# Attention stage of a graph network: visits in pairs of one node block, new orders on four engines, scatters without a bound

## The reference

```python
feat = jnp.concatenate([x[src], edge_weights, x[dst]], axis=1)      # 144 columns
h = jax.nn.relu(feat @ W_att1.T + b_att1)
scores = (h @ W_att2.T + b_att2)[:, 0]
m = jax.ops.segment_max(scores, src, num_segments=num_nodes)
e = jnp.exp(scores - m[src])
denom = jax.ops.segment_sum(e, src, num_segments=num_nodes)
msg = jax.ops.segment_sum((e / denom[src])[:, None] * lin_x[dst], src, num_segments=num_nodes)
```

## Time and profile before

| | us |
|---|---|
| median of 3 runs | 6971.01 |
| runs, lowest to highest | 6955.53 to 6972.53 |
| the profiled execution | 6953.3 |
| its span, first to last instruction | 6951.5 |

### The profile page before, as it was taken

How to read it: one execution, slowest core, us unless ns; L and a number is a source line. 1 busy time by engine, 2 the same in 40 slices (tenths; PEclk the granted TensorE clock), 3 DMA queues, 4 the chain that set the end, 5 groups by cost and what they waited for, 6 DMA issues and landing times.

```text
span 6951.5 us, 172751 instructions
## 1 busy us (share of the span) xinstructions
PE 4916.4 (71%) x30025; PEld 3702.1 (53%) x30026; DVE 4522.2 (65%) x20036; ACT 2115.2 (30%) x5541; POOL 4929.4 (71%) x10449
## 2 busy tenths in 40 slices
PE   6444777777545766676666666666888888888887
PEld 2334444444434544455445444444777777777775
DVE  5777888888434743333333333335999999999997
ACT  4000000000000432222222222223555555555555
POOL 1677777777777367777777777776777777777775
PEclk9555555555555777767877787776888888888888
DMA  8333333333333143333333333334333333333333
GB/s 270 67 60 60 57 60 60 57 60 60 64 60 61 62 133 111 111 110 109 105 106 105 106 106 105 106 105 128 95 94 94 95 95 95 94 94 95 95 95 93
DMA packets 1146496, 649.15 MB, mean 93 GB/s; under 512 B 798450, under 2 KB 1050340, under 8 KB 1145573
## 3 DMA queue, kind: packets, MB, share of 16 engines
q1 hardware_dynamic: 1006804, 412.21, 24.3%
q0 software_dynamic: 137728, 233.30, 11.8%
q10 hardware_dynamic: 1888, 2.83, 0.2%
HBM read 360.75 MB, written 311.42 MB: 97 GB/s over the span
## 4 chain that ended last, share of the span: by engine, by line
issue 19%; PE 15%; POOL 14%; DVE 8%; DMA 4%; ACT 3%; POOLq 1%; DVEq 1%; ACTq 0%; SPq 0%
PE banks L1397 7%; POOL rows_by_src L832 6%; DMA rows_by_src<-ring 3%; PE banks L1443 3%; DVE wide L1991 2%; DVE wide L1996 1%; DVE ring L2002 1%; ACT ring L1085 1%; ACT ring L1092 1%; POOL ring L893 1%; PE banks L1398 1%; PE banks L1385 1%; PE banks L1434 1%; DVE ring L1947 1%; PE banks L1458 1%
## 5 line engine op out<-in xcount | busy, mean ns | idle before, releaser
L832 POOL DMA_INDIRECT rows_by_src<-ring x1760 | 1711.7, 973 | 553.1 <-issue 488.5
L804 POOL DMA_INDIRECT wide<-msg_table,ring x1664 | 1578.8, 949 | 632.1 <-issue 419.4
L1397 PE MATMUL banks<-wide,ring 128*128 x3520 | 1281.9, 492 | 473.6 <-ACT ring L1085 403.4
L1311 PE MATMUL banks<-wide,ring 128*128 x3520 | 859.5, 426 | 505.7 <-DVE acc L1764 190.9
L1397 PEld LDWEIGHTS banks<-wide,ring 128*128 128x128 f32 x3520 | 742.5, 261 | 746.6 <-issue 696.2
L1311 PEld LDWEIGHTS banks<-wide,ring 128*128 128x128 f32 x3520 | 784.7, 328 | 584.0 <-issue 583.5
L1092 ACT COPY ring<-banks 128x416 f32<-128x416 f32 x880 | 402.2, 510 | 1448.8 <-PE banks L1398 1448.8
L1958 DVE COPY ring<-ring 128x4 f32<-128x4 f32 x440 | 80.1, 182 | 1145.5 <-DMA rows_by_src<-ring 1145.4
L1443 PE MATMUL banks<-wide,ring 128*128 x5328 | 708.6, 262 | 0.0
L1764 DVE TENSOR_TENSOR acc<-acc,banks 128x64 f32 x1760 | 388.8, 221 | 366.0 <-DVE acc L1764 201.8
L1443 PEld LDWEIGHTS banks<-wide,ring 128*128 128x128 bf16 x5328 | 544.1, 108 | 114.2 <-issue 0.2
(11 more groups left out here) (326 smaller groups left out, 9426.3 us busy)
## 6 DMA issues: line engine op xcount, KB each, us to landing
wide<-rows_by_src SPq DMA_DIRECT2D x1776, 105.0 KB, 2.0
ring<-attr_turned SPq DMA_DIRECT2D x440, 128.0 KB
attr_turned<-ring SPq DMA_DIRECT2D x416, 96.0 KB
rows_by_src<-ring POOLq DMA_INDIRECT x1760
wide<-msg_table,ring POOLq DMA_INDIRECT x1664
ring<-attr_by_dst SPq DMA_DIRECT2D x208, 64.0 KB
attr_turned<-ring SPq DMA_DIRECT2D x208, 64.0 KB
attr_by_dst<-in_edge_attr_dram SPq DMA_DIRECT2D x1, 13281.2 KB
```

The lines of the kernel that those rows point to most:

```text
L804: g.indirect_dma_start(out=A_g[:, b * GV + u, :], out_offset=None, in_=table[:, :], in_offset=bass.IndirectOffsetOnAxis(ap=A_idx[:, b * GV ...
L832: g.indirect_dma_start(out=rows_d[:, :], out_offset=bass.IndirectOffsetOnAxis(ap=B_pos[:, s, u:u + 1], axis=0), in_=B_row[:, s, u, :], in_ ...
L1311: last = mm(bank[s][:, u * HID:(u + 1) * HID], A_D[:, s, u, :], A_g[:, ds(r[u], 1), :].rearrange("p a k -> p (a k)"), start=True, stop=True)
L1397: mm(b, B_DT[:, t, u, :], qh[:, w, :].rearrange("p a k -> p (a k)"), start=True, stop=False)
```

## The change

The visits of the attention stage come in pairs of one block. A block with an odd number of visits gets one more, whose lanes all lie outside. The stage's table is made for 98 more visits (1872 instead of 1776), so the pipeline has 78 turns of six steps, 468 steps, instead of 74 and 444. The maximum, its correction and the sums are then kept by pair: two columns instead of four, two additions to `acc` instead of four, and TensorE accumulates the two sums of a pair in PSUM. The penalties are worked out once, ahead of the stage (`pens`), and GpSimd copies twelve columns of them once in six steps.

In each engine's `tick` the order is new. On VectorE the comparison moves from the head of the turn behind the scan; on TensorE the transposes of the one-hot matrix move behind the turn of the scores; the product of rows and `C_p` goes from GpSimd (one operation of 128x260) to ScalarE (four of 128x65), and ScalarE's two large copies move to the end of its turn.

For the scatters, the bound goes away. `rows_by_src` gets 16 x 128 spare rows, and a lane outside the block writes the spare row that `aside` names.

The diff, cut to its core:

```diff
-C_VISITS = C_BODY * -(-VISITS // C_BODY)
+C_VISITS = C_BODY * -(-(-(-N_EDGES // P) + N_WIN - 1 + N_WIN) // C_BODY)
+PV = GV // 2
-        rows_d = dram("rows_by_src", [SLOTS, ROW])
+        rows_d = dram("rows_by_src", [SLOTS + BODY * P, ROW])
...
# GpSimd, send
-                            in_=B_row[:, s, u, :], in_offset=None, bounds_check=SLOTS - 1, oob_is_err=False).then_inc(b_sc[s], 16)
+                            in_=B_row[:, s, u, :], in_offset=None).then_inc(b_sc[s], 16)
...
# GpSimd, tick
-                    m_pen = ch.do(g.tensor_tensor(C_pen[:, s, :], wbase_all[:, ds(n, GV)], wbase[:, ds(n, GV)], ALU.subtract))
+                    if s == 3:
+                        after_c(pool, c_new, CS - 1, i, CS)
+                        g.tensor_copy(C_pen, pens[:, ds(i * (CS * PV), CS * PV)]).then_inc(c_pen, 1)
...
-                    m_r = ch.do(g.tensor_tensor(C_r[:, t, :], C_s[:, t, :], sp_[0], ALU.subtract))
-                if 0 in stages:
-                    ch.need(m_pen)
-                    g.tensor_tensor(C_pen[:, s, :], C_pen[:, s, :], C_step, ALU.mult).then_inc(c_pen, 1)
-                if 2 in stages:
-                    ch.need(m_r)
+                    ch.link(g.tensor_tensor(C_r[:, t, :], C_s[:, t, :], sp_[0], ALU.subtract))
...
-                    after_c(pool, c_p, t, j)
-                    after_c(pool, c_ag, t, j, 2)
-                    g.tensor_tensor(C_W[:, t % 2, :, :], C_V[:, t, :, H1:ROW_SRC],
-                                    per_group(C_p[:, t, :], HID + 1), ALU.mult).then_inc(c_W, 1)
...
# ScalarE, tick
+                    after_c(act, c_p, t, j)
+                    after_c(act, c_ag, t, j, 2)
+                    for u in range(GV):
+                        last = a.activation(C_W[:, t % 2, u, :], C_V[:, t, u, H1:ROW_SRC], ACT.Identity, scale=C_p[:, t, u:u + 1])
+                    last.then_inc(c_W, 1)
...
# TensorE, tick: the sums of a pair
-                        last = mm(bank[6 + t % 2][:, u * (HID + 1):(u + 1) * (HID + 1)], C_S[:, t, u, :], C_W[:, t % 2, u, :],
-                                  start=True, stop=True)
+                        last = mm(bank[6 + t % 2][:, (u // 2) * (HID + 1):(u // 2 + 1) * (HID + 1)], C_S[:, t, u, :], C_W[:, t % 2, u, :],
+                                  start=u % 2 == 0, stop=u % 2 == 1)
...
# VectorE, visit_table and rows
+                    ch.link(v.tensor_scalar(ei, t1, 1.0, None, ALU.add))
+                    ch.link(v.tensor_scalar(ei, ei, 1, None, ALU.arith_shift_right))
+                    ch.link(v.tensor_copy(t1, ei))
+                    v.scalar_tensor_tensor(nt[0:K, :], t1, 2.0, hs, ALU.mult, ALU.mult).then_inc(s_vcols, 1)
...
-                    ch.link(v.scalar_tensor_tensor(B_sh[:, s, :], B_rec[:, s, :, 1], -BIG, B_in[:, s, :], ALU.add, ALU.mult))
+                    ch.link(v.tensor_tensor(B_sh[:, s, :], B_rec[:, s, :, 1], aside[:, s, :], ALU.subtract))
+                    ch.link(v.tensor_tensor(B_sh[:, s, :], B_sh[:, s, :], B_in[:, s, :], ALU.mult))
...
+            ch.link(v.tensor_tensor(pens, of_pairs(wbase_all[:, 0:C_VISITS]), of_pairs(wbase), ALU.subtract))
+            v.tensor_scalar(pens, pens, MASKED / P, None, ALU.mult).then_inc(c_init, 1)
```

More of the change, by code:

```diff
@@ L337, in build @@
         C_kl = part(ring, CS * GV // 2, RING).bitcast(bf16).rearrange("p (s u) -> p s u", s=CS)
-        C_mp = part(ring, CS * GV * PARTS // 2, RING).bitcast(bf16).rearrange("p (s u k) -> p s u k", s=CS, u=GV)
-        C_raw, C_s, C_r, C_pen, C_mo, C_mr, C_df, C_cr, C_mg, C_z, C_d, C_p = (marks(CS) for _ in range(12))
-        C_zero, C_step = part(ring, GV, RING), part(ring, GV, RING)
-        C_mn = part(ring, 1 + CS * GV, RING)
+        C_mp = part(ring, CS * PV * PARTS // 2, RING).bitcast(bf16).rearrange("p (s u k) -> p s u k", s=CS, u=PV)
+        C_raw, C_s, C_r, C_mg, C_z, C_d, C_p = (marks(CS) for _ in range(7))
+        C_mo, C_mr, C_df, C_cr = (part(ring, CS * PV, RING).rearrange("p (s u) -> p s u", s=CS) for _ in range(4))
+        C_pen = part(ring, CS * PV, RING)
+        pens = part(ring, C_VISITS // 2, RING)
+        C_zero = part(ring, GV, RING)
+        C_mn = part(ring, 1 + CS * PV, RING)
         at[0] = 0
@@ L1417, in tick @@
                     for u in range(GV):
[L1418 removed]
+                        last = mm(bank[5][:, u * PARTS:(u + 1) * PARTS], C_STb[:, t, u, :], C_mp[:, t, u // 2, :], start=True, stop=True)
                     last.then_inc(c_mm, 1)
@@ L1429, in tick @@
                     last.then_inc(c_MKt, 1)
-                if 0 in stages:
-                    after_c(pe, c_N, s, i)
-                    after_c(pe, c_STc, s, i, 1)
-                    for u in range(GV):
-                        last = tr(bank_b[0][:, u * P:(u + 1) * P], C_N[:, s, u, :], ident_b[:, :])
-                    last.then_inc(c_St, 1)
                 if 1 in stages:
@@ L1451, in tick @@
                     tr(bank_b[1][0:PARTS * GV, 0:P], C_parts[:, t, :], ident_b[:, :]).then_inc(c_pt, 1)
+                if 0 in stages:
+                    after_c(pe, c_N, s, i)
+                    after_c(pe, c_STc, s, i, 1)
+                    for u in range(GV):
+                        last = tr(bank_b[0][:, u * P:(u + 1) * P], C_N[:, s, u, :], ident_b[:, :])
+                    last.then_inc(c_St, 1)
                 if 5 in stages:
```

131 lines of the change are left out of this document (67 added, 64 removed).

## The result

The changed kernel takes 7233.16 us in the median (7225.5 to 7240.5), the kernel before beside it 6971.77: a ratio of 1.038 (95% interval 1.036 to 1.040), 3.8% slower.

The account below looks back on a forecast made before the run. VectorE was taken to set the attention stage's pace, GpSimd's issue rate the scatters'; a ScalarE-GpSimd ring would become the new bound. 6953.3 + 390 - 25 + 2 = 7320, with 17.7 for the median 7338 us; range 7060 to 7420.

Parts of the forecast that it names:

- More steps: Attention stage: 468 steps instead of 444, which at the old pace alone would cost 109 us.
- VectorE's own turn, 4.07: Attention stage: VectorE's work per step falls from 4.54 to 4.07 us; as the bound it would give 1921 us.
- the rival in which the multiplications vanish in ScalarE's idle time: Attention stage: the ring does not close and VectorE stays the bound, 6837 us in all; chance 0.10.
- its 0.47 for two additions: VectorE in the attention stage: dropping two additions to the sums removes spacings of 0.25 and 0.22 us per step.
- The ring of 4.59: Attention stage: ScalarE and GpSimd wait for each other in a closed path, making 4.59 us the step's lower limit.
- The meeting, 0.55: Attention stage: VectorE's comparison holds up a GpSimd operation each step, adding 0.55 us, for a step of 5.14.
- The two paths that were to end 0.01 apart: Attention stage: from the small copy's start, comparison 1.99 us behind and GpSimd's first operation 2.00, so they meet.
- its rival: Attention stage: comparison and GpSimd operation do not meet, the step stays 4.59 us, 7080 in all; chance 0.17.
- Scatters without a bound, 25 of 0 to 49: Edge-row scatters: dropping the bound saves up to 28 ns on each of 1760, 0 to 49 us; 25 taken.
- SP's refills of the rows, costed at nothing: Attention stage: refilling row slots after ScalarE's signal has over 9 us of time, so costs nothing.
- TensorE at its lower level: Attention stage: TensorE stays at 1.2 GHz, its own turn 5.0 us, 7272 in all without the meeting; chance 0.05.
- The 2 us of the tables: Ahead of the attention stage: five small operations and two over 936 columns add an estimated 2 us.

Follow-up runs that it names:

- experiment 9: Changed kernel, ScalarE still multiplying the rows, with the old orders of VectorE, ScalarE and TensorE, row 0 to 127 in SBUF: 6834.73 us, ratio 0.982.
- experiment 12: Changed kernel with old engine orders, ScalarE multiplying, row 0 to 127 in PSUM, and block-number table on partition 0 instead of 64: 6834.12 us, ratio 0.982.
- experiment 1: Changed kernel with the comparison reading the row 0 to 127 from PSUM instead of SBUF: 7041.84 us, ratio 1.011.
- experiment 2: Changed kernel with the comparison reading the row 0 to 127 as 4-byte instead of 2-byte numbers from SBUF: 7226.72 us, ratio 1.038.
- experiment 6: Changed kernel with row multiplication on GpSimd and all engine orders as before, leaving the pairs of visits and scatters without a bound: 7152.97 us, ratio 1.027.
- experiment 7: Changed kernel with GpSimd's row multiplication and all engine orders as before, plus the row 0 to 127 in PSUM: 7162.03 us, ratio 1.027.
- experiment 4: Changed kernel with the row multiplication back on GpSimd and the new orders kept: 7085.09 us, ratio 1.018.
- experiment 8: Changed kernel, ScalarE still multiplying, with the old orders of VectorE, ScalarE and TensorE and the row 0 to 127 in PSUM: 6848.14 us, ratio 0.982.
- experiment 3: Changed kernel with one 128x260 multiplication on ScalarE instead of four of 128x65, all four visits taking the first's weight: 6964.21 us, ratio 1.001.
- experiment 5: Changed kernel with the row multiplication back on GpSimd, new orders kept, and the row 0 to 127 in PSUM: 7047.98 us, ratio 1.010.
- experiment 11: Kernel before the change with the comparison reading the row 0 to 127 from PSUM: 6965.53 us, ratio 0.999.
- experiment 10: Changed kernel with ScalarE's first 128x512 copy put back ahead of the exponentials, all else as changed: 7240.55 us, ratio 1.040.

## Why the prediction was right, and where its sizes were off

The forecast was slower, by a ring through ScalarE and GpSimd with one held operation in each turn, at 7338. It came out slower by that mechanism, at 7233, 105 less. The step accounts for 108 less and the scatters, which gave nothing, for 25 more; the last 22 less are the spread of runs, since the forecast put the median 18 above the profiled execution and it lies 4 below. That the last two nearly cancel is luck. The steps of the prediction:

- **More steps:** 468, as counted.
- **VectorE's own turn, 4.07:** not the bound in the changed kernel. Where the ring is open and VectorE is the bound (experiment 9) a step takes 4.066, and the kernel 6835; the rival in which the multiplications vanish in ScalarE's idle time was priced at 6837. So the condition of that price isn't met in the changed kernel, because of its orders and not because of the multiplications as such. That the price agrees to 2 us is luck: it holds 25 us for the scatters that weren't there, and its 0.47 for two additions is two misses that partly cancel. VectorE in experiment 9:

```profile
5522.34 0.16 DVE L2034 TENSOR_REDUCE ring<-banks 128x4 f32<-128x12 f32 x1
5522.42 0.69 DVE L2038 TENSOR_REDUCE banks<-banks 128x2 f32<-128x512 f32 x1
```

Against the earlier trace rows the time from one of these to the other falls from 0.45 to 0.08 where the prediction took 0.25 away, and that from the scan to the first addition of the node's part from 0.46 to 0.14 (5523.21 to 5523.35) where it took 0.22. On average over the stage the two are worth 0.59, not 0.47, and 0.15 of it goes again into the longer load (experiment 12), which the prediction had put behind the scores.
- **The ring of 4.59:** there, and all its links are seen in the timelines. It measures 4.475 in the median and 4.50 in the mean (experiment 1). Score copies to GpSimd 0.55 (0.56 predicted), GpSimd's chain to the exponential 1.38 (1.35). The mis-sized part is from the exponential to the next score copies, medians over the stage 2.55 instead of 2.68: exponential 0.24 instead of 0.28, multiplications 0.98 instead of 0.96, then in the timeline above 0.14 from the small copy to the first large one (0.21 predicted), 0.63 and 0.57 (0.63, 0.60). The small copy had been sized by the spacing of the two score copies, and the second large copy at 0.60 where the prediction's own rows give 0.67 - 0.09 = 0.58.
- **The meeting, 0.55:** it happens in nearly every turn, as forecast, and costs 0.405. Expected was the first operation, L868; held were L869, L870 or L877, L868 hardly ever (its median stays 202 ns). The two paths that were to end 0.01 apart do not: L868 comes 1.89 behind the small copy's start (2.00 predicted), the comparison 1.96 in the shortest turns (1.99 predicted) but 2.21 in the median and up to 3.05, because VectorE waits for TensorE on the way there (L2005 and L2031 in the waits above). So L868 begins 0.07 to 1.15 ahead of the comparison and gets through, and one of the operations behind it is caught. One that begins later behind the comparison's start loses less: L869, begun 0.16 behind it, loses 0.40, L877, begun 0.20 behind it, 0.35. The prediction allowed for this in a sentence (0.3 to 0.5) and then summed 0.55; the meeting holds over so wide a shift because the chain is longer than the comparison, as the prediction said against its rival. The Trainium skill (GPSIMD Engine Reference, Key points) says that GpSimd contends with VectorE instructions of two SBUF inputs; experiments 1 and 2 agree, 4.50 with one such input and 4.90 with two. Together the two terms, 4.50 and 0.41, make 4.91 instead of 5.14, and 468 x 0.23 = 108 us of the sum.
- **Scatters without a bound, 25 of 0 to 49:** 0. The median is 972 ns with and without a bound, and 1760 of them take 2248.5 us from first to last start (before 2250.9). So the 28 ns against the gather aren't the bound's; whether the length of the rows makes them wasn't tried. VectorE's additional work there (838 busy instead of 783 us) comes out of its waiting, 1075.0 us for landed scatters instead of 1145.4, and costs nothing, as predicted. The Trainium skill (DMA: Bandwidth & Descriptors, Anatomy of one DMA) calls the cost of making descriptors small; the unchanged 972 agrees as far as the bound goes, and what the 972 ns themselves are spent on no run here shows.
- **SP's refills of the rows, costed at nothing:** nothing. GpSimd waits for rows 32.4 us in five cases, 27.4 of it ahead of the first step and the last case 61 us behind it.
- **TensorE at its lower level:** it ran at it more often, 0.75 of full clock in the stage instead of 0.87, and a step from comparison to comparison varies between 4.0 and 5.9 us with it. But it doesn't set the pace. Four successive turns, cut at ScalarE's score copies (the column behind POOL is the clock):

```profile
5407.15:5412.14 4.99, 3.43 (x37) 2.67 (x37) 3.78 (x17) 3.09 (x12) 2.83 (x12) 0.97 0.33 86
5412.14:5416.95 4.81, 4.47 (x34) 4.07 (x35) 3.33 (x15) 3.08 (x12) 2.72 (x12) 0.50 0.36 90
5416.95:5422.11 5.16, 4.10 (x43) 3.51 (x41) 4.33 (x19) 3.09 (x13) 2.67 (x12) 0.83 0.33 83
5422.11:5427.06 4.95, 4.62 (x35) 4.24 (x36) 3.46 (x16) 3.08 (x13) 2.90 (x12) 0.50 0.37 87
```

A turn at 1.2 GHz (0.50) isn't longer than one at 2.4: over the stage the 150 turns with at least three quarters of their time at 1.2 GHz last 4.88 on average, the 139 with as much at 2.4 GHz 4.94. Had I cut the stage at comparisons alone, I would have blamed the clock: there the steps sorted in this way last 5.57 and 4.59 on average; but VectorE only makes up in the latter what it lost in the former.

- **Two rings not foreseen.** The prediction looked for a bound in the changed kernel and found the right one. It said nothing of the pairs alone, and there my expectations (experiments 6 and 7) repeated the step "VectorE sets the pace, so its saved 0.47 is saved time". It isn't: the ring through GpSimd lies close to VectorE's 4.54, and above it with the longer load. ScalarE's multiplication is what opens it: with it, and otherwise the same orders, the step falls from 4.75 (experiment 6) to 4.07 (experiment 9).

The sum with the measured sizes: 468 x 4.91 + 16.6 is 282 over the old stretch, and nothing from the scatters; the two profiled executions differ by 284. The 2 us of the tables can't be told: the first comparison starts at 4804.8 instead of 4801.0, but in the experiments it starts anywhere from 4797 to 4810.

## What to carry to other kernels

Moving work to the engine with the most idle time is decided by where in that engine's order it lands: list, from its waits, who waits for it and whom it waits for, and add up the closed path, because idle time inside such a ring is not room. Here the same change, with the multiplication on the same engine, makes the kernel 1.8% faster with the old orders and 3.8% slower with the new ones. Take the pace from events on the ring itself; steps cut at another engine's event can show a cause that isn't one.

## What the runs showed of the hardware

- A comparison with two inputs in SBUF and a GpSimd operation exclude each other, and whoever begins first goes through: the GpSimd operation ends 0.05 to 0.08 behind the comparison's end (465 cases in the changed kernel), and in experiment 4 the comparison itself waits, up to 1.15 us instead of 0.69. With one of the inputs in PSUM they run side by side at full speed, 0.20 and 0.69 (experiment 1). The Trainium skill (SBUF — State Buffer, SBUF: two separate sides) says that whoever starts first has the shared pair of ports for the whole instruction; the rows agree. I had not counted on the second direction.
- Loading two block numbers into registers takes VectorE 528 ns, on partition 64 as on partition 0 (experiments 8 and 12), loading four from partition 0 344 ns in the kernel before; why was not tried. Behind the scores it is hidden in the changed kernel; where the comparison comes first in the step, the first addition starts 0.93 behind the comparison's start instead of 0.74.
- The granted clock in the attention stage (window 4820 to 6650) goes with the length of the step: 0.95 at 4.07 us (experiment 9), 0.91 at 4.35 (3), 0.79 to 0.88 between 4.50 and 4.59 (1, 4, 5, 11 and the kernel before), 0.76 to 0.78 from 4.75 up (2, 6, 7, 10 and the changed kernel). Which of the two makes the other in these kernels was not separated, except that in the changed kernel the clock doesn't set the turn.
